# A three-stage transformer kernel on one core: order of work in its second turn changed

## The chip, the cores and the metric

One core of a Trainium2 chip. The core has TensorE (PE, matrix products, results in PSUM), VectorE (DVE), ScalarE (ACT), GpSimd (POOL) and the queue that issues transfers (SP); they run side by side and meet at semaphores. The metric is the time of one launch in microseconds on the device; lower is better.

## The reference

Input `x` is 64 sequences of 64 tokens with 256 features, all float32. Four steps are added to it in turn, each behind a layer norm:

```python
x = x + tanh(g_xattn[0]) * attention(layernorm(x), ctx)      # keys and values: the context, then the tokens themselves
x = x + tanh(g_ffn[0])   * dense(layernorm(x))               # silu(x w1) * (x w3), then w2; ternary weights; 682 hidden
x = x + tanh(g_xattn[1]) * wkv(layernorm(x), ctx)            # a recurrence over the 64 tokens, channel by channel
x = x + tanh(g_ffn[1])   * experts(layernorm(x))             # shared part, and the best 2 of 8 experts
```

The recurrence divides one running sum over tokens (weighted values) by another (weights). The experts need a softmax over 8 logits and the two largest of them per token.

## The kernel before

**Blocks and stages.** The 4096 tokens are cut into 8 blocks of 512. Three stages work on three different blocks at a time: "A" (attention and the dense layer) on block i, "W" (recurrence and the choice of experts) on block i-1, "M" (the expert products) on block i-2. One such step is a turn. Turn 0 has A alone, turn 1, the **second turn**, A and W, turns 2 to 7 all three; then `closing` has W and M, and `last` M alone. Each engine has its own hand-written order for each kind of turn, as a Python function of the same name (`turn`, `second`, `closing`, `last`). An engine works strictly in the order written, and waits where a semaphore isn't there yet; everything behind a waiting instruction on that engine waits with it.

**What is shared.** Two PSUM banks, `transit`, carry all small results (transposes, queries, scores, ...) in a fixed order (`TRANSIT`, `SECOND`); one use must be taken out before the next but one comes in. Every chunk of 128 hidden columns, of the dense layer (6, the last a half chunk with 42 + 42 columns, `is_tail`) or of the experts (10), goes through `gate_ps`, `up_ps`, `act_sb`, `hid_h`, `hid_l`, each with two places, so chunk c can start only when chunk c-2 is out:

- PE `up(t, chunk)` (L630) makes the products; it waits until chunk c-2 is gated.
- ACT `squash` (L946) takes the tanh; DVE `gate` (L1417) makes the silu and the product with the second half, in two instructions.
- ACT `high_hidden` (L962) rounds the result; POOL `low_hidden` (L1171) makes the rest, `hid_l`. For the half chunk the rest is made by DVE, `low_tail` (L1428).
- PE `down(t, chunk)` (L659) adds the chunk's part to the sums. DVE `add_sums` (L1405) adds them to the tokens, which the next turn's W takes in.

`f_up(c)` on PE is `up` of dense chunk c and, from c = 2 on, `down` of chunk c-2.

**Attention on DVE:** `row_max` (L1381) gives the maxima of the scores, ACT `softmax` (L904) the exponentials, `row_scale` (L1387) one over their sums, `add_attention` (L1394) adds the result to the tokens. Then a layer norm: DVE `statistics` (L1362), POOL `row_factors` (L1155, four small instructions), ACT `normalise` (L847, four), PE `z_T` (L499, eight transposes), ACT `high_parts` (L855) and DVE `low_parts` (L1374).

**Recurrence on DVE,** for each half h of the 256 channels: `scan_keys` (L1437), `scan_values` (L1441; its input is POOL's `weigh_inputs`, L1165), `add_to_sum`, `add_to_values`, `divide` in two pieces, `quotient` (L1445 to L1464). PE turns the result (`y_T`, L601), DVE adds it to the tokens (`add_recurrence`, L1466), and a layer norm as above follows, with the transposes z3 (`z_T(t, "W", "z3T", ...)`, L793).

**Choice of experts:** PE `route` (L612) makes the logits, ACT `keep_logits` (L938) copies them, PE `logits_T` (L625) turns them back; DVE `route` (L1475) takes the maximum, ACT `route` (L942) the exponential, and DVE goes on with eleven small instructions up to `combine`, which the next turn's M takes in. ACT `keep_rows` (L877) and `keep_context` (L868) save the tokens and the context for the next turn.

**Fillers.** In the second turn PE also multiplies constants (`keep_clock`, L454), 10, 3, 30 and 6 times; each shows as two matmuls in the trace. They stay as they are.

Of the kernel before, what the change touches and what calls it, by code (L numbers as in the profile page):

```python
# [84 lines left out]
def build(nc, x, ctx_in, g_xattn, g_ffn, wqT, wkT, wvT, woT, w1T, w3T, w2T, decay, bonus, router,  # L85
# [8 lines left out]
    KH = D // P  # L94
    HC = -(-HID // P)
# [15 lines left out]
    with ExitStack() as stack:  # L111
# [57 lines left out]
        za_h = sb("za_h", [P, KH, TOK], F32R)  # L169
        za_l = sb("za_l", [P, KH, TOK], F32R)  # L170
# [13 lines left out]
        x2 = sb("x2", [P, NT, D])  # L184
# [266 lines left out]
        def _(pe):  # L451
# [47 lines left out]
            def z_T(t, stage, which, source, n):  # L499
                pe.wait_ge(z_done[stage], t.count(stage, 2, n))  # L500
                for h in range(KH):
                    turn_rows(t, stage, f"{which}{h}", source, h)
# [109 lines left out]
            def route(t):  # L612
                wait_taken(pe, t, "W", "z3T0", "z3T1", claims=("W", "route"))
                if t.fixed and t.i == LAG["W"]:
                    pe.wait_ge(route_in, 16)
                bank, full = claim(t, "W", "route")
                _, z_h, z_l = recurrence_out(t)
                for k in range(KH):
                    for a, z in enumerate((z_h, z_l)):
                        for r in range(NT):  # L620
                            last = nc.tensor.matmul(bank[r * RW:(r + 1) * RW, 0:P], route_w[:, k], z[:, k, r * P:(r + 1) * P].bitcast(F32),  # L621
                                                    start=k == 0 and a == 0, stop=k == KH - 1 and a == 1, tile_position=(0, r * RW))
                last.then_inc(full, 1)

            def logits_T(t):  # L625
                wait_taken(pe, t, "W", "route", claims=("W", "logits"))
                bank, full = claim(t, "W", "logits")
                nc.tensor.transpose(bank[:, 0:P], logitsT, ident[:]).then_inc(full, 1)
# [142 lines left out]
            def second(t):  # L771
                def f_up(c):
                    up(t, ("A", c))
                    if c >= 2:
                        down(t, ("A", c - 2))
                q_and_k(t)
                values(t)
                keys_T(t)
                context_out(t)
                scores(t)  # L780
                keep_clock(10)
                probs_T(t)
                keep_clock(3)
                attend(t)
                keep_clock(30)
                z_T(t, "A", "z1T", za_row, 2)
                keep_clock(6)
                f_up(0)
                y_T(t)
                f_up(1)  # L790
                f_up(2)
                f_up(3)
                z_T(t, "W", "z3T", zw_row, 2)  # L793
                f_up(4)
                route(t)
                f_up(HC - 1)
                logits_T(t)
                down(t, ("A", HC - 2))
                down(t, ("A", HC - 1))

# [39 lines left out]
        def _(act):  # L840
# [6 lines left out]
            def normalise(t, stage, n, rows_in, rows_out, rstd, shift):  # L847

                act.wait_ge(shift_done[stage], t.count(stage, 2, n))
                for r in range(NT):  # L850
                    last = nc.scalar.activation(rows_out[:, r], rows_in[:, r], ACT.Identity, bias=shift[:, r:r + 1],
                                                scale=rstd[:, r:r + 1])
                last.then_inc(z_done[stage], 1)

            def high_parts(t, stage, which, dst, done):  # L855
                for h in range(KH):
                    bank = wait_full(act, t, stage, f"{which}{h}")
                    nc.scalar.activation(dst[:, h], bank[:], ACT.Copy).then_inc(done, 1)
# [79 lines left out]
            def keep_logits(t):  # L938
                bank = wait_full(act, t, "W", "route")
                nc.scalar.activation(logitsT, bank[:, 0:P], ACT.Copy).then_inc(free_of("W", "route"), 1)  # L940

            def route(t):  # L942
                wait_taken(act, t, "W", "logits")
                nc.scalar.activation(pexp[:], pexp[:], ACT.Exp).then_inc(pexp_set, 1)
# [17 lines left out]
            def high_hidden(t, chunk):  # L962
                stage, c = chunk
                pos = CHUNKS.index(chunk) % 2
                if stage == "M" and c >= SC:
                    act.wait_ge(weighted, scaled_chunk(t, c))
                else:
                    act.wait_ge(gated, chunk_no(t, chunk))
                wait_back(act, down_done, t, chunk, 2)
                n = hidden_rows(chunk)  # L970
                nc.scalar.activation(hid_h[0:n, pos], act_sb[0:n, pos], ACT.Copy).then_inc(hid_h_set, 1)  # L971
# [102 lines left out]
            def second(t):  # L1074
                rows = attention_rows(t)
                queries(t)
                own_keys(t)
                normalise(t, "W", 1, x2, zw_row, rstd_w, shift_w)
                values(t)
                key_weights(t)  # L1080
                context_out(t)
                softmax(t)
                probs_T(t)
                normalise(t, "A", 2, rows, za_row, rstd_a, shift_a)
                high_parts(t, "A", "z1T", za_h, za_h_set)
                squash(t, ("A", 0))
                for c in range(1, HC):
                    if c == HC - 1:
                        keep_logits(t)
                    squash(t, ("A", c))  # L1090
                    high_hidden(t, ("A", c - 1))
                    if c == 2:
                        normalise(t, "W", 2, x2, zw_row, rstd_w, shift_w)
                    if c == 3:
                        high_parts(t, "W", "z3T", zm_h, zm_h_set)
                high_hidden(t, ("A", HC - 1))
                keep_rows(t)
                route(t)
                keep_context(t)

            def closing(t):
# [169 lines left out]
        def _(dve):  # L1271
# [109 lines left out]
            def row_max(t):  # L1381
                bank = wait_full(dve, t, "A", "scores")
                nc.vector.tensor_reduce(smax[:], bank[:].rearrange("p (r k) -> p r k", r=NT), AX.X, ALU.max).then_inc(smax_set, 1)
                dve.wait_ge(smax_set, t.count("A", 1, 1))
                nc.vector.tensor_scalar(nsmax[:], smax[:], -SCALE, None, ALU.mult).then_inc(nsmax_set, 1)

            def row_scale(t):  # L1387

                wait_taken(dve, t, "A", "scores")
                nc.vector.reciprocal(rinv[:], psum_row[:]).then_inc(rinv_set, 1)  # L1390
                dve.wait_ge(rinv_set, t.count("A", 1, 1))
                nc.vector.tensor_scalar(rgain[:], rinv[:], gains[:, 0:1], None, ALU.mult).then_inc(rgain_set, 1)
# [208 lines left out]
            def second(t):  # L1601
                rows = attention_rows(t)
                dve.wait_ge(sums_free, t.before(SUMS))
                statistics(t, "W", 1, x2, bn_w, mv_w)
                dve.wait_ge(scan_set, 1)
                scan_keys(t, 0)
                row_max(t)
                scan_keys(t, 1)
                row_scale(t)
                scan_values(t, 0)  # L1610
                add_to_sum(t, 0)
                add_to_values(t, 0)
                scan_values(t, 1)
                divide(t, 0, 0)
                add_attention(t)
                wait_taken(dve, t, "A", "wo0", "wo1")
                statistics(t, "A", 2, rows, bn_a, mv_a)
                divide(t, 0, 1)
                quotient(t, 0)
                add_to_sum(t, 1)  # L1620
                divide(t, 1, 0)
                low_parts(t, "A", "z1T", za_h, za_l, za_h_set, KH, 2 * KH)
                add_to_values(t, 1)
                divide(t, 1, 1)
                quotient(t, 1)
                gate(t, ("A", 0))
                add_recurrence(t)
                wait_taken(dve, t, "W", "yT0", "yT1")
                statistics(t, "W", 2, x2, bn_w, mv_w)
                for c in range(1, HC - 2):  # L1630
                    gate(t, ("A", c))
                low_parts(t, "W", "z3T", zm_h, zm_l, zm_h_set, 0, KH)
                gate(t, ("A", HC - 2))
                gate(t, ("A", HC - 1))
                low_tail(t)
                route(t)
                add_sums(t, "A", gain_f[:, 0:1], rows, x2)

            def closing(t):
# [75 lines left out]
```

## Time and profile before

| | us |
|---|---|
| median of 3 runs (lowest, highest) | 750.08 (749.81, 750.76) |
| the profiled execution, its own time | 751.18 |
| its span | 749.5 |
| PE busy in the span | 711.2 (95%) |
| DVE busy | 517.8 (69%) |
| ACT busy | 362.2 (48%) |
| POOL busy | 331.3 (44%) |

The profile's mean granted clock of TensorE over the whole span is 0.995 of full speed. A timeline row has the start in us from the span's start, the time taken in us, the engine, the line, the operation, what it writes and reads with their shapes, how many instructions are merged, and in brackets the idle time of the engine before it with what ended it. Matmuls overlap: the distance from one start to the next is their pace.

### The profile page before, as it was taken

Reading aid. Unit: us, or ns where it says so; the run is one execution under the profiler, and the core shown is the slowest. Engines: PE = TensorE matmul, PEld = TensorE weight load, DVE = VectorE, ACT = ScalarE, POOL = GpSimd, SP = SyncE. Lnnn points to the kernel's source line nnn. Section 1 sums busy time; section 2 is a strip of 40 time slices with the busy share of each in tenths; the row PEclk is TensorE's granted clock in tenths of the full one; section 3 lists DMA queues with packets and bytes.
Section 4 is the critical chain, followed back from the end, with each engine's and each line's share of the span. In section 5 each row is a group of like instructions: output and inputs, shape, how many; then the busy total and the mean of one; then the engine's idle time right before and its main releaser. Section 6 shows DMA issues by size and latency. Waiting matters only on the chain.

```text
span 749.5 us, 13056 instructions
## 1 busy us (share of the span) xinstructions
PE 711.2 (95%) x4612; PEld 591.8 (79%) x4612; DVE 517.8 (69%) x926; ACT 362.2 (48%) x693; POOL 331.3 (44%) x345
## 2 busy tenths in 40 slices
PE   7998988999999999999999999999999999898896
PEld 6786777788878888788877888787877888687786
DVE  3878396765877478774877478884777668798532
ACT  5664525653366435654365535554456444533221
POOL 2014104534538155443537155362646346276364
PEclk9999999999999999999999999999999999999999
DMA  8240000210112011110012011110012001021121
GB/s 295 73 128 0 1 29 1 67 34 29 58 42 58 15 43 57 57 42 15 27 57 84 14 42 56 54 44 14 28 56 71 27 30 40 1 71 43 58 58 55
DMA packets 31876, 37.04 MB, mean 49 GB/s; under 512 B 2959, under 2 KB 23141, under 8 KB 31845
## 3 DMA queue, kind: packets, MB, share of 16 engines
q1 hardware_dynamic: 31844, 36.63, 15.2%
q8 instruction: 19, 0.31, 0.2%
q14 instruction: 13, 0.10, 0.0%
HBM read 32.30 MB, written 4.33 MB: 49 GB/s over the span
## 4 chain that ended last, share of the span: by engine, by line
PE 63%; DVE 12%; issue 4%; POOL 4%; ACT 1%; DVEq 0%; POOLq 0%; ACTq 0%
PE sums L490 16%; PE gate_ps L490 15%; PE up_ps L490 13%; PE transit L490 7%; PE transit L567 3%; PE transit L482 2%; POOL act_sb L1183 2%; POOL hid_l L1174 2%; PE transit L577 2%; PE transit L597 2%; DVE act_sb L1426 1%; DVE bn_w L1366 1%; DVE act_sb L1424 1%; PE transit L621 1%; DVE wk L1459 1%
## 5 line engine op out<-in xcount | busy, mean ns | idle before, releaser
L1174 POOL TENSOR_TENSOR hid_l<-act_sb,hid_h 128x512 fp32r<-128x512 f32 x120 | 164.0, 1367 | 203.1 <-ACT hid_h L971 202.8
L1424 DVE SCALAR_TENSOR_TENSOR act_sb<-act_sb,gate_ps 128x512 f32<-128x512 f32 (+1 forms) x128 | 86.6, 676 | 112.0 <-ACT act_sb L953 112.0
L971 ACT ACTIVATE hid_h<-act_sb 128x512 fp32r<-128x512 f32 (+1 forms) x128 | 80.3, 627 | 115.9 <-POOL act_sb L1183 79.6
L1183 POOL TENSOR_TENSOR act_sb<-act_sb,late 128x512 f32<-128x512 f32 x64 | 97.7, 1526 | 61.3 <-DVE act_sb L1426 60.5
L490 PE MATMUL sums<-down_h,hid_h 128*128 128x256 f32 x320 | 91.9, 287 | 3.9 <-POOL hid_l L1174 3.9
L490 PE MATMUL sums<-down_h,hid_l 128*128 128x256 f32 x320 | 89.9, 281 | 0.0
L490 PE MATMUL sums<-down_l,hid_h 128*128 128x256 f32 x320 | 89.8, 281 | 0.0
L1426 DVE TENSOR_TENSOR act_sb<-act_sb,up_ps 128x512 f32<-128x512 f32 x120 | 82.4, 687 | 4.1
L953 ACT ACTIVATE act_sb<-gate_ps 128x512 f32<-128x512 f32 x80 | 47.2, 590 | 75.2 <-PE up_ps L490 66.1
L490 PEld LDWEIGHTS sums<-down_h,hid_h 128*128 128x128 f32 x320 | 60.3, 188 | 10.9 <-issue 8.0
L490 PE MATMUL gate_ps<-zm_h,gate_h 128*128 128x512 f32 x140 | 59.9, 428 | 9.2 <-DVE act_sb L1426 9.2
L490 PEld LDWEIGHTS sums<-down_l,hid_h 128*128 128x128 f32 x320 | 60.4, 189 | 2.0
L490 PEld LDWEIGHTS sums<-down_h,hid_l 128*128 128x128 f32 x320 | 60.3, 189 | 0.0
L490 PE MATMUL sums<-w,hid_h 128*128 128x256 f32 x192 | 48.2, 299 | 8.6 <-POOL hid_l L1174 4.5
L490 PE MATMUL gate_ps<-zm_h,gate_l 128*128 128x512 f32 x140 | 55.4, 395 | 0.0
L490 PE MATMUL up_ps<-zm_h,up_h 128*128 128x512 f32 x140 | 55.3, 395 | 0.0
L490 PE MATMUL up_ps<-zm_h,up_l 128*128 128x512 f32 x140 | 55.2, 394 | 0.0
L490 PE MATMUL up_ps<-zm_l,up_h 128*128 128x512 f32 x140 | 55.2, 394 | 0.0
L1459 DVE RECIPROCAL wk<-wk 128x256 f32<-128x256 f32 x32 | 54.9, 1731 | 0.3
L490 PE MATMUL gate_ps<-zm_l,gate_h 128*128 128x512 f32 x140 | 55.1, 394 | 0.0
L953 ACT ACTIVATE act_sb<-gate_ps,half_s 128x512 f32<-128x512 f32 (+1 forms) x48 | 32.7, 681 | 45.0 <-PE up_ps L490 36.6
L490 PEld LDWEIGHTS sums<-w,hid_h 128*128 128x128 f32 x192 | 34.4, 188 | 22.2 <-issue 21.9
(204 smaller groups left out, 1639.3 us busy)
## 6 DMA issues: line engine op xcount, KB each, us to landing
late<-combine_rows SPq DMA_DIRECT2D x64, 256.0 KB, 3.1
ctx_tok<-in_ctx SPq DMA_DIRECT2D x8, 512.0 KB, 4.2
xa<-in_x SPq DMA_DIRECT2D x7, 512.0 KB, 3.5
out_x<-late SPq DMA_DIRECT2D x7, 512.0 KB, 3.0
wk<-in_L_ffn_w SPq DMA_DIRECT2D x2, 682.0 KB
late<-in_L_ffn_w_down SPq DMA_DIRECT2D x1, 1024.0 KB, 7.1
wk<-in_L_ffn_w_gate SPq DMA_DIRECT2D x2, 512.0 KB, 5.1
wk<-in_L_ffn_w_up SPq DMA_DIRECT2D x2, 512.0 KB, 5.0
```

Source lines behind the costliest of these rows:

```text
L482: last = nc.tensor.transpose(bank[:, r * P:(r + 1) * P], source[:, r, h * P:(h + 1) * P], ident[:])
L490: last = nc.tensor.matmul(o, a, b, start=first and n == 0, stop=final and n == len(pairs) - 1, skip_group_check=not group)
L567: last = nc.tensor.matmul(bank[(1 - q) * S:(2 - q) * S, r * D:(r + 1) * D], keys[:, k, 2 * pair + r, 1 + q], wo[:, k], start=k == 0, stop= ...
L577: last = nc.tensor.matmul(bank[q * S:(q + 1) * S, r * P:(r + 1) * P], qo[:, h, (2 * r + q) * S:(2 * r + q + 1) * S], keys[:, h, r, 2 * q:2 ...
L597: last = nc.tensor.matmul(bank[q * S:(q + 1) * S, r * D:(r + 1) * D], probsT[:, cols], vals[:, tile, q], start=True, stop=True)
L953: nc.scalar.activation(act_sb[0:n, pos], gate_ps[pos][0:n], ACT.Tanh, scale=0.5 if stage == "M" else half_s[0:n, 0:1]).then_inc(tanh_done, 1)
L971: nc.scalar.activation(hid_h[0:n, pos], act_sb[0:n, pos], ACT.Copy).then_inc(hid_h_set, 1)
L1174: nc.gpsimd.tensor_tensor(hid_l[:, pos], act_sb[:, pos], hid_h[:, pos].bitcast(F32), ALU.subtract).then_inc(hid_l_set, 1)
L1183: nc.gpsimd.tensor_tensor(act_sb[:, pos], act_sb[:, pos], comb_sb[:, pos], ALU.mult).then_inc(weighted, 1)
L1424: nc.vector.scalar_tensor_tensor(mine, mine, 1.0, gate_ps[pos][0:hidden_rows(chunk)], ALU.add, ALU.mult).then_inc(gated_one, 1)
L1426: nc.vector.tensor_tensor(mine, mine, ups, ALU.mult).then_inc(gated, 1)
L1459: nc.vector.reciprocal(part, part).then_inc(dinv_set, 1)
```

## The change

Three engines get another order in the second turn alone; no instruction is added or taken away.

- PE: the z3 transposes stand ahead of dense chunk 3, not behind it and `down` 1; `route` ahead of chunk 4; `logits_T` ahead of the half chunk.
- ACT: the normalisation of W stands behind `high_hidden` of chunk 0, not of chunk 1; `high_parts` of z3 behind that of chunk 1; `keep_logits` behind that of chunk 3; the exponential `route` ahead of `high_hidden` of the half chunk.
- DVE: both `scan_keys`, `scan_values` and the first `add_to_sum` ahead of `row_max`; the divisions of half 0 ahead of `add_attention`; the work on half 1 close behind attention's statistics; `add_recurrence` ahead of `gate` of chunk 0; `low_parts` of z3 ahead of `gate` 3; `route` between `gate` 4 and `gate` of the half chunk.

```diff
@@ -789,12 +789,12 @@
                 y_T(t)
                 f_up(1)
                 f_up(2)
+                z_T(t, "W", "z3T", zw_row, 2)
                 f_up(3)
-                z_T(t, "W", "z3T", zw_row, 2)
+                route(t)
                 f_up(4)
-                route(t)
+                logits_T(t)
                 f_up(HC - 1)
-                logits_T(t)
                 down(t, ("A", HC - 2))
                 down(t, ("A", HC - 1))
 
@@ -1085,17 +1085,17 @@
                 high_parts(t, "A", "z1T", za_h, za_h_set)
                 squash(t, ("A", 0))
                 for c in range(1, HC):
-                    if c == HC - 1:
-                        keep_logits(t)
                     squash(t, ("A", c))
                     high_hidden(t, ("A", c - 1))
+                    if c == 1:
+                        normalise(t, "W", 2, x2, zw_row, rstd_w, shift_w)
                     if c == 2:
-                        normalise(t, "W", 2, x2, zw_row, rstd_w, shift_w)
-                    if c == 3:
                         high_parts(t, "W", "z3T", zm_h, zm_h_set)
+                    if c == HC - 2:
+                        keep_logits(t)
+                route(t)
                 high_hidden(t, ("A", HC - 1))
                 keep_rows(t)
-                route(t)
                 keep_context(t)
 
             def closing(t):
@@ -1604,36 +1604,37 @@
                 statistics(t, "W", 1, x2, bn_w, mv_w)
                 dve.wait_ge(scan_set, 1)
                 scan_keys(t, 0)
-                row_max(t)
                 scan_keys(t, 1)
-                row_scale(t)
                 scan_values(t, 0)
                 add_to_sum(t, 0)
+                scan_values(t, 1)
+                row_max(t)
                 add_to_values(t, 0)
-                scan_values(t, 1)
                 divide(t, 0, 0)
+                row_scale(t)
+                divide(t, 0, 1)
                 add_attention(t)
                 wait_taken(dve, t, "A", "wo0", "wo1")
                 statistics(t, "A", 2, rows, bn_a, mv_a)
-                divide(t, 0, 1)
-                quotient(t, 0)
                 add_to_sum(t, 1)
                 divide(t, 1, 0)
-                low_parts(t, "A", "z1T", za_h, za_l, za_h_set, KH, 2 * KH)
+                quotient(t, 0)
                 add_to_values(t, 1)
                 divide(t, 1, 1)
+                low_parts(t, "A", "z1T", za_h, za_l, za_h_set, KH, 2 * KH)
                 quotient(t, 1)
-                gate(t, ("A", 0))
                 add_recurrence(t)
                 wait_taken(dve, t, "W", "yT0", "yT1")
+                gate(t, ("A", 0))
                 statistics(t, "W", 2, x2, bn_w, mv_w)
-                for c in range(1, HC - 2):
+                for c in range(1, HC - 3):
                     gate(t, ("A", c))
                 low_parts(t, "W", "z3T", zm_h, zm_l, zm_h_set, 0, KH)
+                gate(t, ("A", HC - 3))
                 gate(t, ("A", HC - 2))
+                route(t)
                 gate(t, ("A", HC - 1))
                 low_tail(t)
-                route(t)
                 add_sums(t, "A", gain_f[:, 0:1], rows, x2)
 
             def closing(t):
```

## Rows read from the trace of the kernel before

**Rows 1.** The page's head.
```profile
span 749.5 us, 13056 instructions
```

**Rows 2.** Windows: busy us of each engine in a stretch, then PEclk, the granted clock.
```profile
core 0: us, PE busy (x) PEld busy (x) DVE busy (x) ACT busy (x) POOL busy (x), PEclk, DMA share, GB/s
139.00:223.00 84.00, 83.45 (x543) 69.60 (x543) 59.59 (x110) 43.39 (x85) 39.67 (x38) 1.00 0.13 42
```

**Rows 3.** Timeline of DVE, second turn, recurrence and attention.
```profile
81.96 2.25 DVE L1439 TENSOR_TENSOR_SCAN wk<-fades,wk 128x520 f32<-128x520 f32 x1 [8.31 <-ACT wk L936]
...
89.45 0.69 DVE L1383 TENSOR_REDUCE smax<-transit 128x4 f32<-128x512 f32 x1 [5.24 <-PE transit L577]
...
90.25 1.23 DVE L1439 TENSOR_TENSOR_SCAN wk<-fades,wk 128x520 f32<-128x520 f32 x1
...
91.97 0.18 DVE L1390 RECIPROCAL rinv<-psum_row 128x4 f32<-128x4 f32 x1 [0.49 <-ACT ctx_tok L908]
...
93.48 0.72 DVE L1449 SCALAR_TENSOR_TENSOR wk<-wk,gamma 128x512 f32<-128x512 f32 x1
...
95.94 1.73 DVE L1459 RECIPROCAL wk<-wk 128x256 f32<-128x256 f32 x1
...
97.58 1.56 DVE L1401 SCALAR_TENSOR_TENSOR late<-transit,rgain,late 128x256 f32<-128x256 f32 x4
...
106.40 1.29 DVE L1378 TENSOR_TENSOR za_l<-transit,za_h 128x512 fp32r<-128x512 f32 x2 [0.42 <-ACT za_h L858]
```

**Rows 4.** Timeline of PE, fillers, z1 transposes, dense chunk 0.
```profile
95.22 6.96 PE L458 MATMUL up_ps<-ones 128*128 128x128 f32 x60
...
105.00 1.09 PE L482 MATMUL transit<-ident,zqo 128*128 128x128 f32 x8 [2.82 <-ACT zqo L851]
...
105.93 2.49 PE L458 MATMUL up_ps<-ones 128*128 128x128 f32 x12
...
108.08 0.77 PE L490 MATMUL gate_ps<-za_h,w 128*128 128x512 f32 x1
...
110.79 1.09 PE L608 MATMUL transit<-ident,vw 128*128 128x128 f32 x8
```

**Rows 5.** Windows, behind two idle stretches of PE.
```profile
106.40:109.70 3.30, 3.30 (x14) 3.01 (x14) 3.30 (x4) 0.38 (x1) 0.00 (x0) 0.51 0.00 0
126.60:130.00 3.40, 1.72 (x14) 1.50 (x13) 1.59 (x3) 2.09 (x4) 1.26 (x1) 1.00 0.00 0
```

**Rows 6.** Timeline of PE, first matmuls of chunk 4, down 2, half chunk.
```profile
121.72 0.48 PE L490 MATMUL gate_ps<-za_h,w 128*128 128x512 f32 x1
...
123.68 0.28 PE L490 MATMUL sums<-w,hid_h 128*128 128x256 f32 x1
...
125.73 0.50 PE L490 MATMUL gate_ps<-za_h,w 128*128 128x512 f32 x1
```

**Rows 7.** Timelines of DVE, POOL, ACT: gate 0 to the normalisation.
```profile
111.65 0.69 DVE L1424 SCALAR_TENSOR_TENSOR act_sb<-act_sb,gate_ps 128x512 f32<-128x512 f32 x1 [0.92 <-ACT act_sb L953]
...
112.98 1.40 DVE L1471 SCALAR_TENSOR_TENSOR x<-transit,gains,x 128x512 f32<-128x512 f32 x2
...
115.08 1.28 POOL L1174 TENSOR_TENSOR hid_l<-act_sb,hid_h 128x512 fp32r<-128x512 f32 x1 [12.24 <-ACT hid_h L971]
...
116.49 0.20 POOL L1158 TENSOR_TENSOR var_w<-mv_w,eps_row 128x4 f32<-128x4 f32 x1
...
117.88 0.20 POOL L1163 TENSOR_TENSOR shift_w<-nmean_w,rstd_w 128x4 f32<-128x4 f32 x1
...
118.28 2.06 ACT L851 ACTIVATE wk<-x,shift_w,rstd_w 128x256 f32<-128x256 f32 x4
```

**Rows 8.** Timeline of DVE, low_tail, route, add_sums.
```profile
129.78 0.69 DVE L1434 TENSOR_TENSOR hid_h<-act_sb,hid_h 64x512 fp32r<-64x512 f32 x1 [0.70 <-ACT hid_h L971]
...
131.21 0.19 DVE L1492 TENSOR_REDUCE psum_e<-pexp 128x4 f32<-128x32 f32 x1 [0.29 <-ACT pexp L944]
...
134.08 1.40 DVE L1413 SCALAR_TENSOR_TENSOR x<-sums,gain_f,late 128x512 f32<-128x512 f32 x2
```

**Rows 9.** Timeline of PE, third turn, expert chunks 0 and 2.
```profile
131.16 0.39 PE L490 MATMUL gate_ps<-zm_h,gate_h 128*128 128x512 f32 x1
...
138.80 0.50 PE L490 MATMUL gate_ps<-zm_h,gate_h 128*128 128x512 f32 x1 [0.91 <-DVE act_sb L1426]
```

## The prediction

> **What bounds the kernel now.** I read the page's head, the windows of TensorE (PE), then the timelines of the only stretch that the change touches, the second turn, on PE from 77.8 to 131.2 us of the span of 749.5 [rows 1]. That execution took 751.18 us, 1.68 around its span, and stands 1.10 above the median of 750.08; the change's effect is worked out in its trace and added to the median. From 139 to 223 us PE is busy 83.45 of 84.00 us at full clock [rows 2]: a late start isn't made up there. So what counts is when PE can run the third turn's expert chunk 2, at 138.80 [rows 9].
>
> In the second turn PE is not the bound. Its 60 filler matmuls end at 102.18, and the transposes of z1 wait 2.82 us [rows 4] for attention's chain: row maxima at 89.45, attention added at 97.58 [rows 3], statistics, GpSimd's factors, ACT's normalisation. From 106.4 to 109.7, 1.4 us after work resumed, the granted clock is 0.51, which is the lower level of 1.2 GHz [rows 5]. There the twelve fillers take 2.15 us up to 108.08, against 1.39 at the pace of the sixty (0.116 each), and dense chunk 0 takes 2.71 (to 110.79 [rows 4]) against 1.96 for chunk 4 [rows 6]. The fall costs 1.51 us.
>
> **Part 1, DVE's front.** Three scans and an add go ahead of row_max, into the 5.24 us of idle before it. A scan alone takes 1.23, an add 0.72, but the scan beside GpSimd's weighting took 2.25 [rows 3]. The second scan now touches the weighting too; I take 2.0 for it and 1.2 for the others, so they run from 84.2 to 89.1 and row_max stays at 89.45: cost nothing. That is the near bound; the far one, all of them slowed as the first, is a row_max 2.4 us late. From 90.25 on stand add_to_values 0.66, divide 1.64 (95.94 to 97.58), row_scale 0.36 (1.51 from 91.97 to 93.48 less a scan's 1.15), divide 1.64 [rows 3]: add_attention at 94.55, just behind PE's first bank of it, instead of 97.58. Statistics, factors and normalisation keep their distances, z1 is ready at 101.97. The fillers, unmoved, end at about 102.1, so the transposes start at 102.12 instead of 105.00. The moved sum and divisions of half 1 fill DVE until 103.4; the low parts start 1.40 behind the transposes, as before, at 103.52, and end at 104.82. Without the idle the clock doesn't fall: chunk 0 runs from 104.87 to 106.83, not from 108.08 to 110.79. **Gain up to here 3.96.**
>
> **Part 2, recurrence before gate 0.** PE turns the recurrence (y_T) from 106.83 to 107.68 and runs chunk 1 to 109.64. DVE adds the recurrence at 107.5; gate 0 follows at 108.95 and ends at 110.35 (before, gate 0 started at 111.65 and the add 1.33 later [rows 7]). Queued behind are the statistics, all gates, and on PE chunk 2, which needs gate 0: 110.40 instead of 109.64, to 112.36. Down 0 runs from 112.53 to 113.56. The statistics run from 110.30 to 112.25; GpSimd has low part 0 (1.28) until 112.39, then its factors, 1.59 as from 116.49 to 118.08 [rows 7], until 114.11.
>
> **Part 3, ACT and PE.** ACT has the normalisation now behind high part 0, ahead of tanh 2. It stands from 111.0 to 114.14 and normalises for 2.06 until 116.20 (before, from 118.28 [rows 7]). Behind it wait tanh 2 (116.1, where 112.6 was possible), high part 1 and on DVE gate 2. PE has the z3 transposes ahead of chunk 3 and stands from 113.56 to 116.25, **2.69 us**. Chunk 3 begins at 117.05, chunk 4 at 121.0 where it stood at 121.72, down 2 at 123.0, by 1.96 for a chunk and 2.05 for a down and route [rows 6]. Of the 3.96 only 0.7 is left.
>
> **Part 4, route before the half chunk.** Tanh 4 comes at 123.2, high part 3 at 123.8, keep_logits ends at 124.6, the logits are turned, and half chunk 5 runs from 124.8 to 125.83. Low part 4 ends at 128.6, down 4 at 129.75. On DVE route follows gate 4 at 125.3 and needs the exponential at 125.8. But on ACT that stands behind tanh 5 and high part 4, 127.15: route resumes at 127.41. It waited 0.29 before; now 1.6. It needs 2.87 more (131.21 to 134.08 [rows 8]), until 130.28, and queued behind it are gate 5 (1.4), its high part (0.70) and low_tail (0.69) [rows 8], for which PE's last down waits. That starts at 133.15, and PE stands from 129.75, **3.40 us**. The third turn's chunk 0 starts at 133.63 instead of 131.16. From there to chunk 2 it was 7.64 with 0.91 of idle for gate 0 [rows 9]. Without that idle (add_sums is at 133.85, was at 134.08, so gate 0 is ready at 138.7) chunk 2 starts at 133.63 + 6.73 = 140.36. **By order alone 1.6 us later**, 751.7.
>
> **The clock.** It fell behind 2.82 of idle [rows 4, 5]; in a window in which PE was busy for only 1.72 of 3.40 us, with 1.68 of idle, it stayed up [rows 5]. The change removes that one gap and makes two, 2.69 with transposes behind it and 3.40, both nearer to the 2.82. PE is the bound behind both, so a fall costs between nothing and the 1.5 measured; I take 1.5, since the matmuls behind are as dense as they were there. Sum: 1.6 + 1.5 + 1.5 = 4.6.
>
> The Trainium skill, "TensorE: Matmul & The Clock Gate", section "Why this matters for your kernels", warns of idle gaps between bursts of matmuls, with a bound that lies a little above 2.82. By it the clock would stay up behind the first new gap and fall behind the second, 753.1. The trace disagrees in that it has a fall behind 2.82.
>
> **Forecast: 754.7 us**, of the added 4.6 a third by order, the rest by clock; chance 0.45, by itself 753.6 to 756.0.
>
> **Rivals.** (a) One fall: the gap of 2.69 is shorter than the only one that led to a fall, and part of the stretch is transposes. 750.08 + 1.6 + 1.5 = 753.2; chance 0.25. None: 751.7; chance 0.08. (b) The third turn absorbs it: its pace could be DVE's, where add_sums is 0.23 earlier, and chunk 2 did wait for DVE (0.91 [rows 9]). 750.08 - 0.2 = 749.9. Against it: PE idles only 0.55 of the 84 us [rows 2]. Chance 0.09. (c) The gap before the z3 transposes doesn't form, and the time is not slower. Price: 2.69 of idle, everything behind moves up by it and half of the later gap's clock stays; 751.7 - 2.7 = 749.0, or a little above with a fall. It decides if ACT can normalise by 111.4, that is, if the factors are ready 2.7 us before my 114.1. For it: before, they were ready at 118.08 and ACT took them at 118.28 [rows 7], so nothing waited. Against it: statistics, factors and normalisation have fixed lengths, and their start hangs on gate 0. Chance 0.10. (d) Something unseen gains over 1.5 us: 0.03.
>
> **How the numbers follow.** A measurement of this kernel tells 0.2% (1.5 us) from no change: 748.6 to 751.6 is same. Faster: (d) and a third of (c) with still more gained, 0.06. Same: the rest of (c), (b), half of the case without a fall, 0.20. Slower: 0.74. The range from 749.6 to 756.2 leaves out (d), most of (c) and the little above two falls, under 0.2 together; the top takes in 1.5 of the 2.4 by which row_max could be late.
>
> **What the changed profile would show.** Right: row_max near 89.4, add_attention near 94.6, the z1 transposes near 102.1 without a wait, no fall of the clock between 102 and 113; two waits of PE, some 2.7 us for ACT at the z3 transposes and some 3.4 for DVE's low_tail at the last down; the third turn's chunk 0 at 133.6 (135.1 with a fall before it) and its chunk 2 between 140.4 and 143.4. Wrong: a normalisation on ACT before 112, a route on DVE that doesn't wait for ACT, a late row_max, or a shift at 139 us that shrinks behind it.

## The result and the profile after

The changed kernel takes **758.43 us** (median of 5, 756.71 to 759.23), the kernel before 750.08 (5 runs, 748.67 to 750.76): ratio **1.0107**, 95% interval 1.0087 to 1.0127. It is slower, as forecast, but by 8.35 us where 4.6 were forecast, and beyond the range's 756.2.

The page's head and its line of TensorE (PE) in the profiled execution, which was the fastest of the five:

```profile
span 755.0 us, 13056 instructions
...
PE 712.3 (94%) x4612; PEld 593.1 (79%) x4612; DVE 520.2 (69%) x926; ACT 361.9 (48%) x693; POOL 331.4 (44%) x345
```

The span is 5.5 us longer, PE's work only 1.1. The timeline of DVE in the front, which answers to [rows 3]:

```profile
81.83 4.34 DVE L1439 TENSOR_TENSOR_SCAN wk<-fades,wk 128x520 f32<-128x520 f32 x2 [8.32 <-ACT wk L936]
86.09 1.21 DVE L1443 TENSOR_TENSOR_SCAN wk<-fades,wk 128x520 f32<-128x520 f32 x1
...
87.86 1.23 DVE L1443 TENSOR_TENSOR_SCAN wk<-fades,wk 128x520 f32<-128x520 f32 x1
89.02 0.66 DVE L1383 TENSOR_REDUCE smax<-transit 128x4 f32<-128x512 f32 x1
...
94.08 1.67 DVE L1401 SCALAR_TENSOR_TENSOR late<-transit,rgain,late 128x256 f32<-128x256 f32 x4
```

Row_max starts at 89.02, attention is added at 94.08. But row_max has no idle before it any more: the scans run without a break into it, and the scores were there earlier, as TensorE's timeline shows (their matmuls at 85.63 take 1.97). It answers to [rows 4, 6, 9]:

```profile
79.98 0.63 PE L513 MATMUL transit<-ident,wk 128*128 128x128 f32 x4 [0.96 <-ACT vals L900]
...
85.63 1.97 PE L577 MATMUL transit<-keys,zqo 128*64 128x128 f32 x32
...
91.53 0.66 PE L586 MATMUL transit<-ident,ctx_tok 128*128 128x128 f32 x4 [1.51 <-ACT ctx_tok L908]
...
102.03 1.09 PE L482 MATMUL transit<-ident,zqo 128*128 128x128 f32 x8 [0.32 <-ACT zqo L851]
...
104.86 0.47 PE L490 MATMUL gate_ps<-za_h,w 128*128 128x512 f32 x1 [0.40 <-DVE za_l L1378]
...
106.81 1.03 PE L608 MATMUL transit<-ident,vw 128*128 128x128 f32 x8
...
110.42 0.50 PE L490 MATMUL gate_ps<-za_h,w 128*128 128x512 f32 x1 [0.70 <-DVE act_sb L1426]
...
116.10 1.09 PE L482 MATMUL transit<-ident,wk 128*128 128x128 f32 x8 [2.42 <-ACT wk L851]
...
133.96 1.19 PE L490 MATMUL sums<-w,hid_h 128*128 128x256 f32 x4 [4.23 <-DVE hid_h L1434]
134.95 0.63 PE L490 MATMUL gate_ps<-zm_h,gate_h 128*128 128x512 f32 x1
...
142.92 0.48 PE L490 MATMUL gate_ps<-zm_h,gate_h 128*128 128x512 f32 x1
```

The z1 transposes at 102.03, chunk 0 from 104.86 to 106.81 and its successors up to chunk 2 came within 0.1 us of the forecast. Both new waits are there too: 2.42 us at the z3 transposes (forecast 2.69) and 4.23 at the last down (3.40). Chunk 0 of the third turn starts at 134.95, not 133.6, and lasts until 139.24, 4.29 us for work that took 2.80 before; chunk 2 starts at 142.92. A third wait is new and was not forecast: 1.51 at 91.53, for the softmax behind row_max (0.16 at this place before).

The timelines of ACT, POOL and DVE at the two new waits, which answer to [rows 7, 8]:

```profile
112.35 0.20 POOL L1158 TENSOR_TENSOR var_w<-mv_w,eps_row 128x4 f32<-128x4 f32 x1
...
127.14 1.26 POOL L1174 TENSOR_TENSOR hid_l<-act_sb,hid_h 128x512 fp32r<-128x512 f32 x1 [1.44 <-ACT hid_h L971]
...
113.97 2.07 ACT L851 ACTIVATE wk<-x,shift_w,rstd_w 128x256 f32<-128x256 f32 x4 [2.94 <-POOL shift_w L1163]
115.95 0.67 ACT L953 ACTIVATE act_sb<-gate_ps,half_s 128x512 f32<-128x512 f32 x1
...
126.96 0.21 ACT L944 ACTIVATE pexp<-pexp 128x32 f32<-128x32 f32 x1
...
125.39 0.19 DVE L1488 TENSOR_TENSOR pexp<-transit,lmax 128x32 f32<-128x32 f32 x1
127.21 0.18 DVE L1492 TENSOR_REDUCE psum_e<-pexp 128x4 f32<-128x32 f32 x1 [1.63 <-ACT pexp L944]
127.31 1.37 DVE L1493 TENSOR_TENSOR wk<-pexp 128x256 f32<-128x256 f32 x1
128.60 0.41 DVE L1494 TENSOR_TENSOR wk<-pexp 128x256 f32<-128x256 f32 x1
...
131.04 0.67 DVE L1424 SCALAR_TENSOR_TENSOR act_sb<-act_sb,gate_ps 64x512 f32<-64x512 f32 x1
...
133.13 0.69 DVE L1434 TENSOR_TENSOR hid_h<-act_sb,hid_h 64x512 fp32r<-64x512 f32 x1 [0.69 <-ACT hid_h L971]
135.19 1.41 DVE L1413 SCALAR_TENSOR_TENSOR x<-sums,gain_f,late 128x512 f32<-128x512 f32 x2 [1.38 <-PE sums L490]
```

ACT normalises at 113.97 (forecast 114.14), 2.94 us idle before, and tanh 2 comes behind it at 115.95. DVE's route waits 1.63 for the exponential, as forecast (1.6). What was not forecast is the next row: the comparison at L1493, the first of route's four 128x256 instructions, takes 1.37 us where its seven sisters in the same trace take 0.41 to 0.42. It runs beside POOL's low part of chunk 4.

Windows of the changed kernel answer to [rows 2, 5]:

```profile
102.00:113.00 11.00, 9.87 (x56) 7.97 (x57) 8.18 (x18) 3.05 (x5) 1.90 (x4) 1.00 0.04 13
...
131.30:138.10 6.80, 4.14 (x12) 3.49 (x13) 4.60 (x9) 2.61 (x4) 0.00 (x0) 0.51 0.03 6
...
145.00:224.00 79.00, 78.44 (x521) 65.48 (x520) 54.59 (x91) 39.61 (x78) 36.95 (x33) 1.00 0.14 41
```

The fall behind the z1 wait is gone (granted clock 1.00 to 113 us). No fall follows the z3 wait in this execution. The one at the last down begins inside the wait and lasts 6.8 us, not 3.3. The third turn is as full as before (78.44 of 79.00 us): nothing is made up.

### The profile page after: what moved, and what is told of

It is laid out like the page before. It is cut to its first block, busy times and chain, and to the rows that moved or that the text cites. A ratio compares the mean times of both kernels' runs of the same rounds, so it can differ in the third digit from the quotient of the medians.

```text
span 755.0 us, 13056 instructions
## 1 busy us (share of the span) xinstructions
PE 712.3 (94%) x4612; PEld 593.1 (79%) x4612; DVE 520.2 (69%) x926; ACT 361.9 (48%) x693; POOL 331.4 (44%) x345
## 4 chain that ended last, share of the span: by engine, by line
PE 64%; DVE 11%; issue 4%; POOL 4%; ACT 2%; DVEq 0%; POOLq 0%; ACTq 0%
PE gate_ps L490 16%; PE sums L490 16%; PE up_ps L490 14%; PE transit L490 7%; PE transit L567 3%; PE transit L482 2%; POOL hid_l L1174 2%; POOL act_sb L1183 2%; PE transit L577 2%; PE transit L597 1%; DVE act_sb L1426 1%; DVE act_sb L1424 1%; ACT hid_h L971 1%; PE transit L621 1%; DVE bn_w L1366 1%
## 5 line engine op out<-in xcount | busy, mean ns | idle before, releaser
L1426 DVE TENSOR_TENSOR act_sb<-act_sb,up_ps 128x512 f32<-128x512 f32 x120 | 82.4, 687 | 4.1
```

The lines of the kernel that those rows point to most:

```text
L1426: nc.vector.tensor_tensor(mine, mine, ups, ALU.mult).then_inc(gated, 1)
```

## The experiments

All ratios are against the kernel before, measured beside the kernel of the row on the same chip (two chips in all, on which its medians were 750.1 to 751.5). "z2 to chunk 2" is the distance on PE from the z2 transposes (80.11 us in the kernel before, 79.98 after) to the third turn's chunk 2, in the one profiled execution; it leaves out what differs in the startup. "Mean clock" is the granted clock's mean over all executions of the kernel.

| kernel | median us (runs) | ratio, 95% interval | z2 to chunk 2 | mean clock |
|---|---|---|---|---|
| before | 750.8 (70, all its later executions) | 1 | 58.69 | 0.996 |
| changed | 758.43 (5) | 1.0107 [1.0087, 1.0127] | 62.94 | 0.991 |
| e1 front | 748.84 (12) | 0.9968 [0.9953, 0.9983] | 54.91 | 0.998 |
| e2 front, middle | 752.15 (12) | 1.0012 [0.9997, 1.0028] | 58.62 | 0.996 |
| e3 front, tail | 756.78 (6) | 1.0077 [1.0054, 1.0100] | 61.41 | 0.990 |
| e4 changed, last wait filled | 754.85 (8) | 1.0048 [1.0032, 1.0064] | 62.92 | 0.998 |
| e5 before, z1 wait filled | 750.09 (12) | 1.0002 [0.9983, 1.0022] | 56.40 | 0.997 |
| e6 changed, exponential early | 757.92 (6) | 1.0088 [1.0058, 1.0117] | 64.46 | 0.990 |
| e7 changed, both waits filled | 753.44 (11) | 1.0052 [1.0035, 1.0069] | 60.95 | 0.998 |
| e8 front, row_max early | 747.66 (12) | 0.9968 [0.9952, 0.9985] | 53.91 | 0.998 |
| e9 front, recurrence first | 746.62 (6) | 0.9943 [0.9921, 0.9965] | 54.88 | 0.998 |
| e10 front, z3 early | 753.03 (12) | 1.0018 [0.9999, 1.0036] | 59.73 | 0.993 |

**The parts one by one: e1, e2, e3.** e1 is the kernel before with only the front's order on DVE:

```diff
                 scan_keys(t, 0)
-                row_max(t)
                 scan_keys(t, 1)
-                row_scale(t)
                 scan_values(t, 0)
                 add_to_sum(t, 0)
-                add_to_values(t, 0)
                 scan_values(t, 1)
+                row_max(t)
+                add_to_values(t, 0)
                 divide(t, 0, 0)
+                row_scale(t)
+                divide(t, 0, 1)
                 add_attention(t)
...
```

> Only DVE's part in front of the recurrence's addition is changed, the rest is the kernel before. If the front's gain of the prediction (3.96 us) is real and was only lost further back, everything behind the z1 transposes moves up by about 4 us: TensorE's third-turn chunk 2 at 134.8 instead of 138.80, time 746.1. If the gain is taken in by another wait of the second turn even without the other two parts, 750. If the whole slowdown comes from the front, 755 or more.

e2 is the changed kernel with the choice of experts put back on all three engines. e3 is e1 with the choice of experts moved as in the change, except that PE's `route` stays behind chunk 4 and only `logits_T` moves; ACT's `keep_logits` has the same place in both orders, in front of tanh 5. DVE's part of e3 against e1:

```diff
                 gate(t, ("A", HC - 2))
+                route(t)
                 gate(t, ("A", HC - 1))
                 low_tail(t)
-                route(t)
```

> Front and middle (recurrence added before gate 0, normalisation ahead of tanh 2, z3 transposes ahead of chunk 3) as in the changed kernel, the choice of experts where it was before. If the tail (route before the half chunk) is what costs, TensorE's last down comes directly behind the one before it, near 129.9, chunk 2 of the third turn near 138, and the time is 749 to 751, the last with a fall of the clock at the z3 wait. If the middle is what costs, 755 or more.

> Front as changed, middle as before, route before the half chunk as changed. If front and tail add up by themselves: the front's 4 us gained, the tail's wait of TensorE (4.2 us in the changed kernel) and its clock fall paid: last down about 131, chunk 2 about 138.5 without and 140.5 with the fall, time 750 to 752. If the loss needs both parts, about 746. If the tail is worth more than it seems (falls at every run), 753 or more.

The front gains 2.1 us (748.84 against 750.91, the kernel before measured beside it), not 4. The middle on top costs 3.3 (e2 against e1), the tail 7.9 (e3 against e1). e2's time lies between its two cases. e3 fell to its last case, a tail worth more than it seemed: from z2 to chunk 2 it takes 6.5 us more than e1 (61.41, 54.91), with the same wait of 4.22 at the last down. e1's miss is in the baseline: its chunk 2 is 3.78 us earlier than in the profiled execution of before, but the medians differ by little over half of that.

**Is the profile of before typical? e5.** The only edit is `keep_clock(42)` for `keep_clock(30)` in front of the z1 transposes.

> The kernel before with 24 more filler matmuls (2.8 us) in TensorE's 2.82 us wait in front of the z1 transposes. Nothing is computed sooner. Theory: the profiled execution of the kernel before had a clock fall there (1.5 us), and the prediction counted its removal as a gain of the front. If it happens in nearly every run, the median falls by 1.5 us, to 749.4; if the profiled execution was a rare draw, the median stays within 0.4 us of the kernel before. The front alone (748.84) should still be faster than this, by what its order gives at full clock: 1 to 1.7 us.

In the median nothing was gained (0.3 us, 748.1 against 748.4, if the spans are compared, since some executions of e5 spent up to 1.1 us more outside theirs). Yet the fillers do keep the clock up in some executions: the mean clock was 0.999 or 1.000 in 4 of e5's 12 and never above 0.998 in the 70 of the kernel before, while the shortest spans are 746.6 and 746.8. So this fall cost little even where it happened. The profiled execution of e5 had no fall at all (mean clock 1.000), and shows what the profile of before hid. Timeline of PE, then of DVE:

```profile
80.20 0.63 PE L513 MATMUL transit<-ident,wk 128*128 128x128 f32 x4 [0.96 <-ACT vals L900]
...
103.40 1.09 PE L482 MATMUL transit<-ident,zqo 128*128 128x128 f32 x8
...
109.19 1.09 PE L608 MATMUL transit<-ident,vw 128*128 128x128 f32 x8 [0.86 <-DVE vw L1464]
...
136.60 0.50 PE L490 MATMUL gate_ps<-zm_h,gate_h 128*128 128x512 f32 x1 [0.95 <-DVE act_sb L1426]
...
82.05 2.25 DVE L1439 TENSOR_TENSOR_SCAN wk<-fades,wk 128x520 f32<-128x520 f32 x1 [8.31 <-ACT wk L936]
87.85 0.69 DVE L1383 TENSOR_REDUCE smax<-transit 128x4 f32<-128x512 f32 x1 [3.54 <-PE transit L577]
...
95.97 1.56 DVE L1401 SCALAR_TENSOR_TENSOR late<-transit,rgain,late 128x256 f32<-128x256 f32 x4
...
108.44 0.69 DVE L1464 TENSOR_TENSOR vw<-wk 128x512 f32<-128x512 f32 x1
```

Row_max stands 7.65 us behind the z2 transposes, in the kernel before 9.34 [rows 3]. There the context product ran at the low clock, a fall that the prediction left out (windows of the kernel before):

```profile
82.30:85.70 3.40, 3.40 (x19) 1.91 (x20) 1.91 (x1) 0.60 (x1) 2.88 (x2) 0.51 0.00 0
```

Its 32 matmuls took 5.36 us, 3.67 in e5, and so 1.7 us of what looked like idle for the scans was TensorE's lateness. In the changed kernel row_max is at 9.04, since the scans fill DVE. So at full clock the front delays row_max by 1.4 us, and brings the z1 transposes forward not by 2.9 but by 1.15 (22.05 for 23.20). A fall in the context product costs the new order little: e4 and e6 had one in their profiled executions, and their z1 transposes stand 22.40 and 22.41 us behind z2, against 24.89 in the kernel before. The front gains 1.15 us there in executions without this fall and 2.5 in those with it.

The other fall of the profile before, behind the z1 wait, hid less. In the kernel before `y_T` stands at 110.79 [rows 4], right behind DVE's `quotient` 1:

```profile
110.04 0.69 DVE L1464 TENSOR_TENSOR vw<-wk 128x512 f32<-128x512 f32 x1
```

In e5 chunk 0 is done sooner, and TensorE then waits 0.86 us for `quotient` 1. From z2 to `y_T` it takes 30.68 us before and 28.99 in e5: the difference, 1.69, is the context product's fall alone. Of the 1.51 us behind the z1 wait 0.6 came back later, where gate 1 and low part 1 were late for dense chunk 3 and `down` 1: the z3 transposes stand at 40.81 before and 38.51 in e5.

**Order against clock: e4 and e7.** Both are the changed kernel with fillers in its waits; e4 has those ahead of the last down only.

```diff
                 f_up(2)
+                pe.wait_ge(gated, chunk_no(t, ("A", 1)))
+                keep_clock(9)
                 z_T(t, "W", "z3T", zw_row, 2)
...
                 down(t, ("A", HC - 2))
+                keep_clock(15)
                 down(t, ("A", HC - 1))
```

> The changed kernel with 30 more filler matmuls (3.5 us) in the 4.23 us in which TensorE waits for its last down. Nothing is computed sooner, so only the clock can change. If the clock is part of the slowdown as predicted, the fall at 131 to 138 us is gone, the third turn's chunk 0 takes 2.8 instead of 4.3 us, and the time falls by 2.0 us (0.5 for the last down, 1.5 for chunk 0), to about 756.4. If the clock is no part of it, the time stays at 758.4.

> The changed kernel with 30 filler matmuls in the wait at the last down and 18 in the wait at the z3 transposes (behind a wait for gate 1, which is done by then). Theory: what is left is order alone; runs at a mean granted clock of 0.998 to 1.0, the second-turn part of the time as in the runs at full clock with the last wait alone filled (753.8 to 754.5), median 754.2 and the scatter smaller. If the z3 wait never costs a clock fall, it is as with the last wait alone filled, 754.85; if the first fillers delay the z3 transposes, more.

e4 is 3.6 us faster than the changed kernel (2.0 were expected), e7 5.0, and in 7 of e7's 11 executions the mean granted clock was 1.000, in none of the changed kernel's five above 0.993. Timeline of PE in e7, whose profiled execution had no fall either:

```profile
80.08 0.63 PE L513 MATMUL transit<-ident,wk 128*128 128x128 f32 x4 [0.96 <-ACT vals L903]
...
102.12 1.09 PE L482 MATMUL transit<-ident,zqo 128*128 128x128 f32 x8 [0.32 <-ACT zqo L854]
...
116.17 1.09 PE L482 MATMUL transit<-ident,wk 128*128 128x128 f32 x8 [0.26 <-ACT wk L854]
...
134.02 0.71 PE L490 MATMUL sums<-w,hid_h 128*128 128x256 f32 x4 [0.87 <-DVE hid_h L1437]
134.57 0.39 PE L490 MATMUL gate_ps<-zm_h,gate_h 128*128 128x512 f32 x1
...
137.34 1.03 PE L482 MATMUL transit<-ident,ctx_tok 128*128 128x128 f32 x8
...
141.03 0.48 PE L490 MATMUL gate_ps<-zm_h,gate_h 128*128 128x512 f32 x1
```

The last down and chunk 0 take 0.55 and 2.77 us, where the changed kernel took 0.99 and 4.29: this fall cost 2.0. The z3 wait brings a fall in some executions; e4's own had one (PE's windows), and its chunk 2 stands 1.97 us behind e7's. Whether filling this wait too gains time is not clear from the medians: e4 and e7 differ by 1.4 us, of which 0.65 lies outside the spans (752.45 and 751.7), and their ratios, 1.0048 and 1.0052, don't differ.

```profile
117.00:121.00 4.00, 3.84 (x14) 3.41 (x15) 2.67 (x4) 2.39 (x5) 1.27 (x1) 0.57 0.02 4
```

e5 and e7 have the two orders at full clock throughout. Their spans are 747.0 and 751.6, their distances from z2 to chunk 2 56.40 and 60.95: **the order costs 4.6 us**. The other executions at 1.000 agree: a span of 747.1 in e5, 751.1 to 752.6 in e7.

**The tail's terms: e6.** ACT's exponential (`route(t)`) stands directly behind `keep_logits(t)`, ahead of tanh 5.

> The changed kernel with one ScalarE instruction moved: the choice of experts takes its exponential ahead of the half chunk's tanh, not behind it and a rounding. Theory A (the wait for the exponential, 1.63 us, and the comparison of 1.37 instead of 0.42 us, which ran beside GpSimd's low part, are two terms of the tail): both go, TensorE's wait at the last down shrinks from 4.2 to about 1.7 us, time 2.6 us less by order, and another 1.5 to 2 where the clock no longer falls: 754 to 756. Rival (the length of route itself sets the loss): less than 1 us.

The wait for the exponential went from 1.63 to 0.30 us, and the wait at the last down from 4.23 to 2.99. But the slow instruction only changed its name. DVE's and POOL's timelines:

```profile
127.64 0.19 DVE L1492 TENSOR_REDUCE psum_e<-pexp 128x4 f32<-128x32 f32 x1 [0.30 <-ACT pexp L944]
127.74 0.41 DVE L1493 TENSOR_TENSOR wk<-pexp 128x256 f32<-128x256 f32 x1
128.08 0.42 DVE L1494 TENSOR_TENSOR wk<-pexp 128x256 f32<-128x256 f32 x1
128.53 0.43 DVE L1495 TENSOR_TENSOR wk<-wk,before 128x256 f32<-128x256 f32 x1
128.99 1.45 DVE L1496 TENSOR_TENSOR wk<-wk 128x256 f32<-128x256 f32 x1
...
128.90 1.26 POOL L1174 TENSOR_TENSOR hid_l<-act_sb,hid_h 128x512 fp32r<-128x512 f32 x1 [1.44 <-ACT hid_h L971]
```

Now the sum of comparisons (L1496) takes 1.45 us, beside the low part of chunk 4, where it took 0.43 in the changed kernel. The clock fell here three times in the second turn, and the median is only half a microsecond lower. The fall at the last down now costs more: last down and chunk 0 take 6.07 us together, 5.28 in the changed kernel and 3.32 in e7, since more of it lies behind the shorter wait. So expectation A held for the exponential and failed for the comparison and for the time, which is as the rival said (less than 1 us): 1.2 us of order are shown in the trace, not in the median.

**The middle's terms: e9, e10.** e9 is e1 with `add_recurrence` ahead of `gate` 0; e10 is e1 with the normalisation, the z3 transposes and the low parts early, and gate 0 first.

> The kernel with the front alone changed, plus the recurrence added before gate 0 on VectorE; ScalarE and TensorE as before. If the late gate 0 alone is what the middle costs (3.3 us between the medians with and without the middle), the time is 752. If, as the prediction has it, it costs TensorE only its wait for gate 0 (0.7 us) and the rest is the normalisation's place, 748.9 to 749.6, and TensorE has a wait of 0.7 us at chunk 2 and none at the z3 transposes.

> The kernel with the front alone changed, plus the normalisation ahead of tanh 2 on ScalarE, the z3 transposes ahead of chunk 3 on TensorE and the z3 low parts ahead of gate 3; gate 0 stays ahead of the recurrence's addition. If the place of the normalisation and the transposes is the cost, TensorE waits 2.4 us or more at the z3 transposes, chunk 2 of the third turn comes 2.5 to 3.5 us later counted from the z2 transposes (54.9 with the front alone), and the time is 751.5 to 752.5. If the cost needs the late gate 0, 749.

e9 costs nothing, where 0.7 us were expected: 54.88 us from z2 to chunk 2, 54.91 in e1, although e9's profiled execution had the fall in the context product and so its z1 transposes 0.28 later behind z2 (22.32, 22.04). TensorE's 0.70 at gate 0 are there, but PE then waits neither for low part 0 ahead of `down` 0 (0.83 in e1) nor for gate 1 ahead of chunk 3 (0.23). Its median of 746.62 is below e1's, in executions at 746.0 to 746.6 with clock 1.000; e1's three at 1.000 took 746.7 to 747.1. e10 has the whole cost of the middle: 4.82 us more than e1 from z2 to chunk 2, fall included (2.5 to 3.5 were expected), and a median of 753.03, 0.5 above what was expected. Its PE timeline and windows:

```profile
120.40 1.97 PE L482 MATMUL transit<-ident,wk 128*128 128x128 f32 x8 [2.71 <-ACT wk L851]
```

```profile
119.30:126.20 6.90, 5.80 (x19) 5.03 (x20) 2.66 (x4) 3.71 (x8) 1.28 (x1) 0.51 0.00 0
```

**Row_max with the scores: e8.** It is e1 with row_max behind three scans, the divisions of half 0 behind attention's statistics, the z1 low parts ahead of `quotient` 0, `y_T` behind chunk 1, and 29 for 30 fillers.

> The kernel with the front alone changed, but row_max behind three scans instead of all four and one sum; attention is added before the divisions, the z1 low parts before the last division, the recurrence's transposes on TensorE behind chunk 1, two filler matmuls fewer. Theory: with no clock fall in the context product, row_max stands 1.4 us behind the scores because VectorE is still scanning, a loss that the profile before could not show. If so, row_max comes with the scores, the z1 transposes 1.5 us earlier counted from the z2 transposes (20.5 instead of 22.0), third-turn chunk 2 1.3 to 1.6 us earlier, and the time 1.4 us under the front alone, 747.4. Rival: another wait (attention's product, VectorE's later divisions) takes it in, and the time stays at 748.8.

The z1 transposes come 20.28 us behind z2, 22.04 in e1. Of the 1.76, 1.00 arrives at chunk 2 (53.91): TensorE now waits 1.38 for gate 1 ahead of dense chunk 3, where e1 waits 0.23. The median is 747.66 (747.4 expected), but the kernel before measured beside it was lower as well: the ratio is e1's, so the time shows no gain over e1. Both e8 and e9 beat both kernels; 746.62, e9, is the lowest median here.

## Why the prediction was right in direction and wrong in size

**Parts 2 and 3 held.** Gate 0, the factors at 113.94, the normalisation at 113.97, the z3 transposes 0.15 us from where they were forecast: "stands from 113.56 to 116.25" was 113.68 to 116.10. e9 and e10 show the cause to be the one given, the place of the normalisation and the transposes, not gate 0.

**Part 1 failed at "Cost nothing" for the scans ahead of row_max, and at "Gain up to here 3.96".** The scans had the length I gave them. The idle that should have covered them, 5.24 us, was 3.54 at full clock (e5, row at 87.85), because the profiled execution of before had a fall at 82.3 to 85.7 that the text never looked at. At full clock chunk 0 starts 24.88 us behind z2 in the changed kernel and 26.03 in e5, 1.15 gained. The 3.96 was taken one step further, at `y_T`: there it is 26.83 against 28.99, 2.16 gained, since the work on half 1, done sooner, also ends `y_T`'s wait. Of that 1.49 reach the third turn's chunk 2 (e1 54.91, e5 56.40). The rest of the 3.96 was the context product's fall, 1.69. The 1.51 that the text gave to the fall behind the z1 wait were no gain at `y_T`, where `quotient` 1 was the later one; filling that wait (e5) gained nothing in the median.

**Part 4 was mis-sized by one term.** The exponential's wait was right. The 2.87 us for the rest of route was read where POOL stood still; beside its low part one instruction takes 1.37 instead of 0.42, 0.95 more.

**"By order alone 1.6 us later" set a full-clock plan against a profile with two falls.** Counted from z2, the forecast had chunk 2 at 60.25 (140.36 - 80.11) against 58.69. Measured at full clock it is 60.95 (e7) against 56.40 (e5). The plan of the changed order was 0.7 off: the comparison's 0.95, less 0.27 because chunk 2 follows chunk 0 after 6.46 us in e7 (134.57 to 141.03), not 6.73. The baseline was 2.3 off: 1.69 for the context product's fall (5.36 less 3.67) and 0.6 of the 1.51 behind the z1 wait. So the order costs 4.55, not 1.6.

**The clock term was the larger miss.** On the same account, with the 2.3 of the baseline's falls taken as clock, the forecast was 3.9 by order and 3.0 - 2.3 = 0.7 by clock. One minus the mean granted clock, times the time, is 3.2 us per execution before (0.9957 over 70 executions) and 6.5 after (0.9914 over 5). That counts low clock in idle time too, but the spans give the same net: the median span is 749.0 before, 2.0 above e5's two executions at 1.000, and 756.7 after, 5.2 above the median of e7's seven. The net is 3.2 to 3.3, not 0.7, and 4.6 + 3.3 = 7.9 of the 8.35 measured; the last 0.4 is within the intervals. "A fall costs between nothing and the 1.5 measured" failed too: the last down's cost 2.0 in the changed kernel, since it lasts 6.8 us, of which TensorE was busy for 4.14, and 2.7 in e3 and e6 (last down and chunk 0 together 6.02 and 6.07 us, 3.32 in e7). The z3 wait has a fall in some executions (e2, e4, e6, e10) and in others not (changed kernel); the rest falls in other turns or at the z2 transposes (e4, e6, e9), where the prediction had none.

The Trainium skill's "TensorE: Matmul & The Clock Gate", section "Why this matters for your kernels", advises against idle gaps of over about 3 us between bursts of matmuls; by it the clock would have stayed up behind the shorter wait. The changed kernel's profiled execution agrees (up behind 2.42 us, down in 4.23), e4's disagrees: its fall at 117 followed a wait of 2.41 us.

**Rivals.** (a), one fall, is what the second turn of the profiled execution had, but at 2.0 us and with an order that costs 4.6. (b) and (c) didn't happen: the third turn was full, and the z3 gap formed.

Open: where the falls outside the second turn come from (657 to 661 us in the changed kernel) and why some kernels have more of them. No run was made on it. Nor is there a run that keeps route away from POOL's low part, so the comparison's 0.95 is read in the traces and not confirmed by a time.

## What to carry to other kernels

A profile is one execution. Before costs are read from it, look where the granted clock was low in it, and take those stretches out of the baseline on both sides: an idle that a slow stretch makes is no room for moved work, and a removed fall is only a gain where no other engine holds up the same step. Fillers in the waits give two orders at full clock, whose spans can then be compared directly. And a DVE instruction with both inputs in SBUF that is moved beside POOL's large elementwise work has to be priced there, not where it stood.

Of the moves themselves: work moved ahead of an in-order engine's next task must be ready when that engine gets there. The normalisation and the route were each moved in front of the work that the bound needed next, and each waited for its input with everything behind it.

## What the runs showed of the hardware

A 128x256 elementwise operation of DVE from and to SBUF took 0.41 to 0.43 us alone and 1.36 to 1.45 beside a 128x512 operation of POOL of 1.26 (changed kernel, e3, e6): it ended 0.3 us after POOL's. Its inputs were in SBUF; the gate's product (L1426), with one input in PSUM, took 0.69 us beside POOL's low part (changed kernel, 117.37) as elsewhere. The granted clock went to its lower level inside a wait of TensorE and stayed there for 6.8 us although TensorE was busy for 4.14 of them (in e10 5.80 of 6.90), twice the 3.3 of the falls in the profile before; in e3 it stayed for 10.2 us (128.7 to 138.9). Executions of one kernel had mean granted clocks between 0.991 and 0.998 (before) or 0.993 and 1.000 (e8), and went with them in time.
